# Three small products of a graph network kernel, made over all 128 rows with the unused rows zeroed

## The reference, cut to what matters

```python
# SAGE, layer l of 3: sums of neighbours, divided by their number
h   = relu(x @ Wp.T + bp)
agg = segment_sum(h[src], dst, N)
cnt = segment_sum(ones(E), dst, N)
x_l = agg / maximum(cnt, 1)[:, None] @ Wl.T + bl + x @ Wr.T

# the second block's graph network, its head
h = relu(layernorm(message_feats @ W1 + b1, gamma, beta))
h = relu(h @ W2 + b2)              # h has 128 features, W2 is 128 x 512
```

## Time and profile before

| | us |
|---|---|
| runs | 1699.32, 1695.72, 1695.84 |
| median of the runs | 1695.84 |
| span of the profiled execution | 1690.6 |
| TensorE busy | 1555.0 (92% of the span) |
| VectorE busy | 989.6 (59%) |
| ScalarE busy | 445.7 (26%) |
| GpSimd busy | 305.1 (18%) |

### The profile page before, as it was taken

The page is one execution under the profiler, slowest core; times in us unless marked ns, Lnnn a source line. Parts: engine busy times, 40 slices in busy tenths (PEclk is TensorE's granted clock), DMA queues, the critical chain, the costliest instruction groups (busy, mean ns, idle before and its releaser), DMA issues.

```text
span 1690.6 us, 23793 instructions
## 1 busy us (share of the span) xinstructions
PE 1555.0 (92%) x8983; PEld 1214.2 (72%) x8983; DVE 989.6 (59%) x1767; ACT 445.7 (26%) x854; POOL 305.1 (18%) x191
## 2 busy tenths in 40 slices
PE   4798988897999999999998999998999999898998
PEld 3686877776777777877786788877757755676765
DVE  7878767889954672397256666665154511763332
ACT  4423111223311220130124242434215101441222
POOL 1000002053111031004001222212211000004565
PEclk9899998999999999999998999999999999899999
DMA  5122324341230020011001010100101322529343
GB/s 158 45 71 91 105 88 164 118 146 52 88 114 27 1 69 25 1 50 68 25 1 51 25 50 26 50 25 26 51 14 53 115 86 80 206 71 316 55 80 44
DMA packets 52138, 123.93 MB, mean 73 GB/s; under 512 B 8417, under 2 KB 28792, under 8 KB 44894
## 3 DMA queue, kind: packets, MB, share of 16 engines
q1 hardware_dynamic: 14026, 65.34, 11.3%
q10 hardware_dynamic: 28147, 46.81, 8.0%
q0 software_dynamic: 9856, 10.28, 3.5%
HBM read 92.87 MB, written 40.22 MB: 79 GB/s over the span
## 4 chain that ended last, share of the span: by engine, by line
PE 75%; DVE 11%; DMA 5%; issue 3%; ACT 3%; POOL 1%; PEld 0%; DVEq 0%; ACTq 0%; PEldq 0%; SPq 0%; POOLq 0%
PE ps L620 9%; PE ps L621 9%; PE ps L622 9%; PE ps L2288 6%; PE ps L678 4%; PE ps L680 4%; PE ps L631 4%; PE ps L632 4%; PE ps L633 4%; PE ps L939 3%; PE ps L3045 3%; PE ps L3067 3%; PE ps L826 2%; DMA d_w<-arena 2%; DMA arena<-d_w 2%
## 5 line engine op out<-in xcount | busy, mean ns | idle before, releaser
L620 PE MATMUL ps<-wslot,XH 128*125 128x512 f32 (+2 forms) x560 | 214.9, 384 | 5.4 <-DVE XL L1456 3.9
L621 PE MATMUL ps<-wslot,XH 128*125 128x512 f32 (+2 forms) x560 | 212.9, 380 | 0.0
L622 PE MATMUL ps<-wslot,XL 128*125 128x512 f32 (+2 forms) x560 | 212.6, 380 | 0.0
L2936 POOL CAST wslot<-arena 128x2048 fp32r<-128x2048 f32 x25 | 47.7, 1908 | 798.3 <-PEq L3013 428.5
L631 PE MATMUL ps<-XH,wslot 128*128 128x500 f32 (+1 forms) x336 | 123.2, 367 | 17.6 <-DVE XL L1456 10.6
L1461 DVE TENSOR_TENSOR arena<-ps,arena 125x512 f32<-125x512 f32 x150 | 98.2, 684 | 51.3 <-PE ps L622 45.3
L620 PEld LDWEIGHTS ps<-wslot,XH 128*125 128x125 f32 x560 | 104.8, 187 | 31.3 <-issue 4.4
L678 PE MATMUL ps<-CTr,Hhi 125*128 125x500 f32 (+1 forms) x360 | 125.0, 361 | 0.0
L632 PE MATMUL ps<-XH,wslot 128*128 128x500 f32 (+1 forms) x336 | 121.8, 362 | 0.0
L633 PE MATMUL ps<-XL,wslot 128*128 128x500 f32 (+1 forms) x336 | 120.9, 360 | 0.0
L622 PEld LDWEIGHTS ps<-wslot,XL 128*125 128x125 f32 x560 | 104.6, 187 | 22.7
(11 more groups left out here) (445 smaller groups left out, 3074.7 us busy)
## 6 DMA issues: line engine op xcount, KB each, us to landing
arena<-in_units SPq DMA_DIRECT2D x29, 1024.0 KB, 4.8
arena<-in_units SPq DMA_DIRECT2D x8, 2048.0 KB, 11.8
d_w<-arena ACTq DMA_DIRECT2D x10, 625.0 KB
d_wt<-arena ACTq DMA_DIRECT2D x10, 625.0 KB, 4.1
rows<-in_rows ACTq DMA_DIRECT2D x22, 256.0 KB, 4.0
d_kv<-V SPq DMA_DIRECT2D x20, 250.0 KB
arena<-d_kv SPq DMA_DIRECT2D x20, 250.0 KB
arena<-d_wt ACTq DMA_DIRECT2D x2, 2441.4 KB
```

Of the source, the lines that this page charges most:

```text
L620: pe.matmul(o, lhsT=xh[:, k, s], rhs=H4[:, k, 0:nw], start=k == 0, stop=False, skip_group_check=True)
L621: pe.matmul(o, lhsT=xh[:, k, s], rhs=L4[:, k, 0:nw], start=False, stop=False, skip_group_check=True)
L622: last = pe.matmul(o, lhsT=xl[:, k, s], rhs=H4[:, k, 0:nw], start=False, stop=k == K - 1, skip_group_check=True)
```

## The change

The three products keep their columns and their number, and are made over 128 rows in place of 16, 8 and 64.

- `heavy_c`, `heavy_h` and `heavy_h3` are zeroed by GpSimd over all 128 rows. Rows 0 to 15 are written afterwards as before, by the same instructions.
- The counts' product takes as its stationary operand 0.5 in 128 rows (a new constant, `ones_r[:, 2:4]`), since all 16 rows of `heavy_c` now count, which hold the values twice.
- The bias of the head is held in 64 rows high and 64 rows low, with 1/64 as the constant.

The memsets: `heavy_c` (1250 columns) behind the ten scatters of unit 4; `heavy_h` and `heavy_h3` (384 and 128 columns) in front of unit 6's split. They raise the semaphore `zeroed`, which a DMA has already brought to 16, to 17 and to 19; VectorE waits for 17 before L1597 and for 19 before each of the three L1491.

```diff
-        ones_r = sb("ones_r", [128, 2], F32R)
+        ones_r = sb("ones_r", [128, 4], F32R)
...
-        heavy_rows = [heavy_h[0:16, 128 * m:128 * m + 128] for m in range(3)] + [heavy_h3[0:16, :]]
+        heavy_rows = [heavy_h[:, 128 * m:128 * m + 128] for m in range(3)] + [heavy_h3[:, :]]
...
-                    pe.matmul(o, lhsT=heavy_rows[i % KC], rhs=heavy_c[0:16, c0:c0 + w], start=False, stop=True,
+                    pe.matmul(o, lhsT=heavy_rows[i % KC], rhs=heavy_c[:, c0:c0 + w], start=False, stop=True,
...
-                pe.matmul(o, lhsT=ones_r[0:8, 0:1].to_broadcast([8, 128]), rhs=heavy_c[0:8, c0:c0 + w], start=False,
+                pe.matmul(o, lhsT=ones_r[:, 2:3].to_broadcast([128, 128]), rhs=heavy_c[:, c0:c0 + w], start=False,
...
-                    pe.matmul(o, lhsT=ones_r[0:64, 1:2].to_broadcast([64, TP]), rhs=HH[0:64, 1, 0:D], start=False, stop=True,
+                    pe.matmul(o, lhsT=ones_r[:, 1:2].to_broadcast([128, TP]), rhs=HH[:, 1, 0:D], start=False, stop=True,
...
-            act.activation(ones_r[:, 1:2], ones2[:, 1:2], ACT.Copy, scale=1.0 / 32)
+            act.activation(ones_r[:, 1:2], ones2[:, 1:2], ACT.Copy, scale=1.0 / 64)
+            act.activation(ones_r[:, 2:4], ones2[:, 0:2], ACT.Copy, scale=0.5)
...
-            act.activation(HH[0:64, 1, 0:D], row("gnnb2")[0:64, :], ACT.Copy).then_inc(hg_high, 1)
+            act.activation(HH[:, 1, 0:D], rows[:, ROW_SLOT["gnnb2"], :], ACT.Copy).then_inc(hg_high, 1)
...
                 o = mx_wait(dve, (f"h{l}", 0))
+                dve.wait_ge(zeroed, 19)
                 own(dve.tensor_copy(heavy_h[0:16, :], o[0:16, 0:384]))
...
             dve.wait_ge(heavy_rounded, 1)
+            dve.wait_ge(zeroed, 17)
             dve.tensor_tensor(heavy_c[0:16, :], heavy_raw, heavy_top[32:48, :].bitcast(F32), ALU.subtract)\
...
-                own(dve.tensor_tensor(HH[32:64, 1, 0:D], rows[32:64, ROW_SLOT["gnnb2"], :], HH[32:64, 1, 0:D].bitcast(F32),
+                own(dve.tensor_tensor(HH[64:128, 1, 0:D], rows[64:128, ROW_SLOT["gnnb2"], :], HH[64:128, 1, 0:D].bitcast(F32),
...
+                elif u == 6:
+                    pool.memset(heavy_h[:, :].bitcast(F32), 0.0).then_inc(zeroed, 1)
+                    pool.memset(heavy_h3[:, :].bitcast(F32), 0.0).then_inc(zeroed, 1)
...
                             .then_inc(heavy_scattered, 16)
+                    pool.memset(heavy_c[:, :].bitcast(F32), 0.0).then_inc(zeroed, 1)
```

## The result

The changed kernel takes 1683.8 us (median of 4 runs, 1681.12 to 1685.77) against 1697.58 for the kernel before, measured beside it (4 runs): ratio 0.9921 with a 95% interval of 0.9902 to 0.9941, 13.4 us less by that ratio (10.0 to 16.6). Timed again in more rounds it was 0.9925 (0.9908 to 0.9942). The forecast was 14.8 us less and 1681.0, in a range of 1677.5 to 1686. The span of the profiled execution went from 1690.6 to 1679.4 us.

A forecast was written before the change was run, and what follows sets the result against it. TensorE's matmuls were taken to bound the kernel, fully busy in the aggregations. Aggregations 13.7 plus counts 1.1 made 14.8 us, head and zeroing 0: 1695.84 - 14.8 = 1681.0 us, range 1677.5 to 1686, chance 0.78.

The forecast's parts named there:

- The surcharge: TensorE's extra time before and behind a closing product of few rows among larger ones: 0.37 to 0.39 us per occurrence.
- the 96-row neighbour: Shared expert's closing product over 96 rows beside 128-row ones: 0.23 us steps in and out, so no extra cost.
- 36 x 0.38 = 13.7 us in the aggregations: Aggregations' 36 closing products over 16 rows: 0.38 us saved each, 13.7 us, all on the path; bounds 0 to 14.0.
- The counts, 1.1 us: Three closing products of the counts: 0.38 us saved each, 1.1 us on the path; bounds 0 to 1.2.
- The head, 0: Head's ten bias products: TensorE's saving counted as 0, as it waits for VectorE and ScalarE; head-pays rival 0.06.
- the most that the head could save, 5.4 us: Upper bound for the head's ten products: 2.3 us at full clock plus at most 3.1 us at half clock.
- The zeroing and the waits, 0: GpSimd's memsets and VectorE's new waits: hidden, 0 us; bounds for the zeroing 0 to 1.2 us.
- a load can't run under a matmul of the same rows: Rival on TensorE's weight loads: 128-row products would wait like 16-row ones, nothing won, 1695.8 us; chance 0.06.
- half of the surcharge stays: Rival at the closing products: the step out keeps 0.2 us, 7.8 of 14.8 us stay, 1688.6 us; chance 0.07.
- GpSimd's queue makes it slower: Rival: `heavy_c`'s memset outlasts GpSimd's free 5.01 us before unit 5's split, delaying the end; 1700 us; slower 0.03.
- The low clock, which I had as a bound of the change: In the head: with TensorE idle longer, ten us more at half clock would cost 5 us, giving 1686, the range's top.
- The 5.24 us that I put down to "what lies around the span": Median of runs above the profiled span of 1690.6 us, for what lies around it and between runs; carried over unchanged.

The follow-up runs named there:

- e5: The changed kernel without its head part, with the aggregations' and counts' closing products over 64 rows instead of 128; ratio to the kernel before 1.0014.
- e6: The changed kernel without its head part, with the aggregations' and counts' closing products over 65 rows instead of 128; ratio to the kernel before 0.9923.
- e2: The changed kernel with the head's bias product back over 64 rows, aggregations and counts over 128; ratio to the kernel before 0.9922.
- e3: The kernel before with only the head's bias product made over 128 rows; ratio to the kernel before 1.0007.
- e4: The kernel before plus only the memsets, new waits and third constant, all products as before; ratio to the kernel before 0.9997.
- e7: The kernel before with its 16-row aggregation product placed first in every second job, so two follow each other; ratio to the kernel before 0.9966.
- e8: The kernel before with each 16-row aggregation product split in two of about half the columns; ratio to the kernel before 1.0006.
- e1: The changed kernel again, unaltered, timed in more rounds; ratio to the kernel before 0.9925.

## Why the prediction was right

- **The surcharge is the rows'.** Forecast from the 96-row neighbour; e5 and e6 place the limit between 64 and 65. The columns of the stationary operand don't do it: where products with 16 of them (`h0`, 125*16) meet products with 128 (`ag0`, 125*128), in the kernel before, the step is 501.16 - 500.93 = 0.23 us.
- **36 x 0.38 = 13.7 us in the aggregations, all on the path.** G became 13.7 us shorter in both traces of the changed kernel and in e2, and TensorE stayed busy throughout the first layer's stretch.
- **The counts, 1.1 us.** The jobs lie 0.44 us closer where 0.38 was said. From the first count's product to the first of `h0` were 496.55 - 458.91 = 37.64 us, and it is 495.26 - 458.83 = 36.43 now: 1.2 us, at the upper bound that I gave, for 1.1 said.
- **The head, 0.** e3 says -0.04 to +0.19%, H is shorter by 0.1 us, and TensorE's waits in it grew by 4.3 us for the 4.6 that its products saved. The waits did not grow where I had said: ahead of the first product of `head_out(1)` VectorE's wait is 1.00 us for 1.14, and it was the transposes before it, which wait for ScalarE, that took up time (2.3 for 1.5). What I had as the most that the head could save, 5.4 us, was too much: at half clock the surcharge is 0.59 us and not 0.78, so 2.3 + 2.4 = 4.7.
- **The zeroing and the waits, 0.** e4: 0.9997. The row that I trusted for this, a VectorE subtraction beside a memset at its usual duration, held: beside the new memset the two-operand instructions keep their 0.75 us. ScalarE's bias copy takes 0.63 us over 64 rows and over 128, and VectorE's subtraction 0.68 over 32 rows and 0.69 over 64.

```profile
398.88 0.75 DVE L1451 SCALAR_TENSOR_TENSOR arena<-arena,small,rows 125x512 f32<-125x512 f32 x1
```

- **The rivals.** That a load can't run under a matmul of the same rows is refuted by the loads above: 128 rows load under 125. So is the sentence of the Trainium skill beside it ("TensorE: Matmul & The Clock Gate", "Part 3: Packing small matmuls — row/col tiling"), that a load overlaps a matmul in flight only when their row groups differ, if it is taken by itself; the same section also lets a load into a background weight buffer go ahead, and the loads above don't contradict that. What fits the surcharge is another page of the Trainium skill, "TensorEngine Tiling (Array Packing)", section "Tiling Modes": changing the tiling mode drains TensorE, with modes for 64 rows and for 32. The threshold of e5 and e6 and the switches of e7 agree with it. That the engine drains can't be read from a trace; what the rows show is a load that starts only with its own matmul, and 0.38 us for going and coming back. That half of the surcharge stays, and that GpSimd's queue makes it slower, did not happen (steps of 0.22 us on both sides; 3.25 us still free).
- **Two sums of the prediction.** With half of the surcharge kept, the time would have been 1681.0 + 7.8 = 1688.8 us and not 1688.6; and 4 x 0.23 is 0.92, which makes the head's surcharge 0.40 us. Neither enters the forecast.
- **What was off: the span.** The profiled spans differ by 11.2 us, 3.6 less than forecast, while G and the counts give 14.9. The other 3.7 us are given back outside the changed products. From the logits' first product to the rank product (L1021) the profiled execution of before took 1502.3 - 1482.0 = 20.3 us, the shortest of all ten traces; the changed kernel's took 22.5, and the kernels with the old head 22.0 (e2), 24.9 (e4), 22.1 (e5), 23.2 (e6), 21.8 (e7) and 23.1 (e8). With the new head e1 and e3 took 22.3 and 21.9. The low clock, which I had as a bound of the change, reaches into the logits with either head, but not at the same place. In the kernel before it lay on the first group of logits, behind which TensorE waited for ScalarE in any case (1.12 us), and the second group ran at full clock (start, duration, instruction):

```profile
1482.55 0.62 PE L1002 MATMUL ps<-XH,wgL 128*16 128x500 f32 x1
1482.97 0.62 PE L1004 MATMUL ps<-XL,wgH 128*16 128x500 f32 x1
```

  In the changed kernel's trace the first group ran at full clock, TensorE waited 3.05 us behind it, and the low clock lay on the second group, from 1474.76 to 1477.8, behind which it does not wait. The second group has the low clock in all nine other traces, with the old head as with the new, and only the trace of before has it on the first group; what decides where it falls stays open.

```profile
1474.76 0.76 PE L1000 MATMUL ps<-XH,wgH 128*16 128x500 f32 x1
1475.32 0.62 PE L1002 MATMUL ps<-XH,wgL 128*16 128x500 f32 x1
...
1478.11 0.38 PE L1004 MATMUL ps<-XL,wgH 128*16 128x500 f32 x1
1478.33 0.38 PE L1000 MATMUL ps<-XH,wgH 128*16 128x500 f32 x1
```

  Steps of 0.42 us at half clock and 0.22 at full. That makes 2.2 of the 3.7 us. Of the rest, 1.2 lie between the shared expert's first product (L1043) and the end: 179.2 us before, 180.4 after, 178.2 to 179.8 in the other kernels. The last 0.3 us are spread.
- **The 5.24 us that I put down to "what lies around the span".** In the changed kernel's runs it is 1681.12 - 1679.4 = 1.7 us, and as much in the later runs of the kernel before. The profiled execution of before was shorter than the median by the other 3.5 us. Carrying the difference over to the median was right; most of it was scatter between runs. The median of before is itself 1.7 us higher in the final measurement (1697.58 against 1695.84), which is part of why 1683.8 lies 2.8 us above 1681.0.
- **What stays open.** The four measurements with the full gain (first, e1, e2, e6) give 12.7 to 13.4 us less. Each interval holds 14.8, and yet all four values lie below it. That G and the counts are worth 14.9 us is shown by the traces; whether the whole time gets all of it, or gives a us or two back behind the third layer, is not shown.

## What to carry to other kernels

A small product wedged between full ones is not priced by its size but by whether TensorE has to change over for it: look at the steps into and out of it, and compare with a product of another row count in the same position. If it has 64 rows or fewer between products of more, try 65 or more rows (zeros, or the operand repeated and scaled), which cost nothing here, and keeping several small ones together saves the switches without any zeroing. It pays only where TensorE sets the pace: in the head the same edit on ten products gave nothing.

## What was not expected

- The threshold is as sharp as one row: 64 rows step at 0.32, 0.41 and 0.33 us, 65 rows at 0.23, 0.22 and 0.23.
- Two small products in a row (e7) are 0.33 us apart, not 0.23. The four steps from 507.69 to 508.98 around the pair take 1.29 us, where four common ones take 0.90: 0.39 us for a pair as for a single one, but 0.10 of it stands between the two. The rows of a single small product show the same 0.10 us in another place: behind the first large product after it the step is 0.33 us too (510.39 to 510.72 in e5). So each change of rows costs about 0.10 us ahead of the first product behind it and about 0.10 us behind that product. With a single small product the 0.10 us behind it and the 0.10 us ahead of the next large one fall on the same step, the 0.41 us; with a pair they fall on two.
- Executions of one kernel differ by up to 8 us before the first aggregation alone: it starts at 499.9 us in one trace of the changed kernel and at 507.9 in the other, and the other eight lie between. A change of 1 us can be read in a stretch of the trace and not in the time.
